# Five features of the last two tiles looked up by one-hot products instead of gathered, and a layer moved behind tile 14

## The reference

```python
e = stack([tbl_f[ids[:, f]] for f in range(26)], axis=1)       # 2048 x 26 x 128
combined = concatenate([dense[:, None, :], e], axis=1)           # 27 vectors a sample
dots = einsum('bfd,bgd->bfg', combined, combined)[:, IU0, IU1]   # its 351 pairs
h = concatenate([dense, dots, dense], axis=1)                    # 607 numbers
h = maximum(h @ W_top1 + b_top1, 0)                              # 512
h = maximum(h @ W_top2 + b_top2, 0)                              # 256
y = h @ W_top3                                                   # 1
```

## Time and profile before

| | us |
|---|---|
| median of 3 runs | 379.87 |
| lowest, highest | 377.62, 384.15 |
| span of the profiled execution, first to last instruction | 496.1 |
| TensorE busy in it | 376.0 |
| VectorE, ScalarE, GpSimd busy in it | 244.4, 195.0, 254.8 |
| mean granted TensorE clock, as a share of full speed | 0.904 |

### The profile page before, as it was taken

The page is one execution under the profiler, slowest core; times in us unless marked ns, Lnnn a source line. Parts: engine busy times, 40 slices in busy tenths (PEclk is TensorE's granted clock), DMA queues, the critical chain, the costliest instruction groups (busy, mean ns, idle before and its releaser), DMA issues.

```text
span 496.1 us, 8109 instructions
## 1 busy us (share of the span) xinstructions
PE 376.0 (76%) x3360; PEld 301.4 (61%) x3360; DVE 244.4 (49%) x174; ACT 195.0 (39%) x261; POOL 254.8 (51%) x266
## 2 busy tenths in 40 slices
PE   1951777858586665978798796969788696879997
PEld 1630656647474554767586666867676455666787
DVE  4740789674919370765725750956566101112133
ACT  3810986414242521525252532434354334344400
POOL 6774540655737363646666554747466564730000
PEclk9985799989989796989998898989899898789899
DMA  8841763259915153456714533536232621123330
GB/s 210 218 134 41 218 187 85 70 156 275 227 29 161 45 155 103 109 150 153 183 46 128 160 87 104 143 93 193 74 89 63 168 73 27 49 63 100 69 71 5
DMA packets 38479, 58.44 MB, mean 118 GB/s; under 512 B 21665, under 2 KB 22561, under 8 KB 38444
## 3 DMA queue, kind: packets, MB, share of 16 engines
q1 hardware_dynamic: 29304, 40.74, 30.3%
q0 software_dynamic: 8192, 16.79, 13.5%
q10 hardware_dynamic: 948, 0.41, 0.4%
HBM read 47.68 MB, written 10.23 MB: 117 GB/s over the span
## 4 chain that ended last, share of the span: by engine, by line
PE 58%; issue 16%; DVE 11%; another core or an unknown queue 8%; SPq 3%; DMA 2%; ACT 2%; DVEq 0%; ACTq 0%
PE look_bank L727 25%; PE short_bank L821 15%; DVE one_hot L1031 8%; PE out_bank L757 6%; PE out_bank L771 4%; PE short_bank L806 4%; PE out_bank L766 3%; SPq L632 2%; DVE all_combined L1044 1%; DVE low_table L1019 1%; DMA spread_ids<-in_ids_by_feature 1%; PE out_bank L783 1%; SPq L621 1%; DMA last_scratch<-all_dots 1%
## 5 line engine op out<-in xcount | busy, mean ns | idle before, releaser
L682 POOL DMA_INDIRECT rows<-in_tbl,all_ids x256 | 253.9, 992 | 191.9 <-PE short_bank L821 81.9
L1031 DVE TENSOR_TENSOR one_hot<-spread_ids,row_bank 128x2048 fp32r<-128x2048 int32 (+3 forms) x80 | 170.7, 2175 | 27.1 <-PE look_bank L727 10.7
L727 PE MATMUL look_bank<-one_hot,high_table 125*128 125x512 f32 x328 | 140.8, 429 | 20.0 <-issue 16.1
L727 PE MATMUL look_bank<-one_hot,low_table 125*128 125x512 f32 x328 | 132.4, 404 | 0.6 <-issue 0.6
L821 PE MATMUL short_bank<-all_combined 128*59 128x54 f32 x2048 | 88.1, 247 | 53.2 <-issue 51.5
L821 PEld LDWEIGHTS short_bank<-all_combined 128*59 128x59 f32 x2048 | 79.7, 162 | 66.7 <-issue 66.5
L1044 DVE COPY all_combined<-short_bank 128x512 f32<-128x512 f32 x32 | 21.8, 691 | 156.2 <-PE short_bank L806 122.3
L727 PEld LDWEIGHTS look_bank<-one_hot,high_table 125*128 125x128 f32 x328 | 64.5, 197 | 40.5 <-issue 23.6
L727 PEld LDWEIGHTS look_bank<-one_hot,low_table 125*128 125x128 f32 x328 | 64.6, 197 | 16.9 <-issue 4.1
L925 ACT COPY all_dots<-short_bank 128x432 f32<-128x432 f32 x64 | 33.1, 518 | 97.1 <-remote 53.7
L878 ACT COPY looked_up<-look_bank 128x512 f32<-128x512 f32 x40 | 23.4, 586 | 120.8 <-remote 45.3
(11 more groups left out here) (42 smaller groups left out, 183.5 us busy)
## 6 DMA issues: line engine op xcount, KB each, us to landing
whole_table<-in_tbl SPq DMA_DIRECT2D x26, 448.0 KB
spread_ids<-in_ids_by_feature SPq DMA_DIRECT2D x40, 256.0 KB
block_scratch<-all_dots SPq DMA_DIRECT2D x24, 208.0 KB
rows<-in_tbl,all_ids POOLq DMA_INDIRECT x256
block_scratch<-all_dots SPq DMA_DIRECT2D x24, 104.0 KB
pairs<-block_scratch SPq DMA_DIRECT2D x72, 29.2 KB
whole_table<-in_tbl SPq DMA_DIRECT2D x26, 52.0 KB
whole_table<-in_tbl SPq DMA_DIRECT2D x2, 560.0 KB
```

What stands on the lines that cost most here:

```text
L682: nc.gpsimd.indirect_dma_start(rows[:, t % ROW_TILES, slot, :], None, tables[SLOT_FEATURES[slot]][:, :], bass.IndirectOffsetOnAxis(ap=all_ ...
L727: last = nc.tensor.matmul(look_bank[s % LOOK_BANKS][:], table_parts[part][TABLE_PLACE[s]][0:ROWS_K, c, :], one_hot[0:ROWS_K, (chunks_befor ...
L1031: last = nc.vector.tensor_tensor(one_hot[:, place:place + n, :], spread_ids[:, s % ID_PLACES:s % ID_PLACES + 1, :].to_broadcast([P, n, COLS]),
```

## The change

Tiles 14 and 15 gather only slots 0 to 10, in groups of 4, 4 and 3. Slots 11 to 15 (five tables of 1250 rows, ten chunks each) become lookups 40 to 44 for these two tiles together, in 256 columns. TensorE does eight of their ten halves behind tile 12 and two behind tile 13. Their tables are loaded, cast and split like the others; ScalarE copies the results into the place of block 2's (`copy_late`) and moves five for tile 14 behind lookup 44, five for tile 15 behind tile 14 (`move_late`), for which the dots of these tiles wait. Of block 2's layers, six steps of layer 1 stay behind tile 12, ten stand behind tile 13, and layer 2 stands behind tile 14, where the last transposes of tile 15 now come before the third layer. The places for ids go from seven to five. The core of the diff:

```diff
-LOOK_FEATURE = [SLOT_FEATURES[GATHERED[m] + LOOK_SLOT[s]] for s, m in enumerate(BLOCK_OF)]
+LATE_LOOKS, LATE_TILES = 5, 2
+ALL_LOOKS = LOOKS + LATE_LOOKS
+LATE_SLOT = GATHERED[LAST] - LATE_LOOKS
+FIRST_LATE = TILES - LATE_TILES
+LATE_COLS = LATE_TILES * P
+LOOK_FEATURE = ([SLOT_FEATURES[GATHERED[m] + LOOK_SLOT[s]] for s, m in enumerate(BLOCK_OF)]
+                + SLOT_FEATURES[LATE_SLOT:GATHERED[LAST]])
...
-ID_PLACES = 7
+ID_PLACES = 5
 LOOK_PLACES = 15
 SPLIT_AHEAD = 2
-AGAIN = [m > 0 and s - FIRST_LOOK[m] < TABLE_PLACES for s, m in enumerate(BLOCK_OF)]
+AGAIN = [m > 0 and s - FIRST_LOOK[m] < TABLE_PLACES for s, m in enumerate(BLOCK_OF)] + [False] * LATE_LOOKS
 TABLE_PLACE = []
-for s, m in enumerate(BLOCK_OF):
-    TABLE_PLACE.append(s if s < TABLE_PLACES else TABLE_PLACE[2 * FIRST_LOOK[m] - 1 - s if AGAIN[s] else s - TABLE_PLACES])
+for s in range(ALL_LOOKS):
+    TABLE_PLACE.append(s if s < TABLE_PLACES else
+                       TABLE_PLACE[2 * FIRST_LOOK[BLOCK_OF[s]] - 1 - s if AGAIN[s] else s - TABLE_PLACES])
 HIGH, LOW = range(2)
-GROUPS = [[4, 4, 4, 4] for _ in range(BLOCKS)]
+GROUPS = [[4, 4, 4, 4]] * FIRST_LATE + [[4, 4, 3]] * LATE_TILES
+assert all(sum(sizes) == (LATE_SLOT if t >= FIRST_LATE else MOST_GATHERED) for t, sizes in enumerate(GROUPS))
...
+LATE_HALVES_AFTER = {LAST * PER_BLOCK: 8, LAST * PER_BLOCK + 1: 2}
+LATE_OUTS_AFTER = [6, 10]
...
-        return [out_steps(LAST - 1)[:12], out_steps(LAST - 1)[12:-1], [],
+        first = 2 * LOOKS + sum(LATE_HALVES_AFTER.get(i, 0) for i in range(t))
+        looks = [step for half in range(first, first + LATE_HALVES_AFTER.get(t, 0)) for step in look_steps(half)]
+        outs, (a, b) = out_steps(LAST - 1)[:-1], LATE_OUTS_AFTER
+        return [merge(looks, outs[:a], 1.0), merge(looks, outs[a:a + b], 0.5), outs[a + b:],
...
-        ahead = ahead[:-1] + out_steps(LAST - 1)[-1:] + out_steps(LAST)[:4] + ahead[-1:]
+        return ahead[:-1] + work_after(t) + ahead[-1:] + out_steps(LAST - 1)[-1:] + out_steps(LAST)[:4]
...
-                sp.dma_start(spread_ids[:, i, :], ids_by_feature[s:s + 1, :].to_broadcast([P, COLS])).then_inc(
+                n = look_cols(s)
+                sp.dma_start(spread_ids[:, i, 0:n], ids_by_feature[s:s + 1, COLS - n:COLS].to_broadcast([P, n])).then_inc(
...
-                if s + TABLE_PLACES < LOOKS and not AGAIN[s + TABLE_PLACES]:
+                if s + TABLE_PLACES < ALL_LOOKS and not AGAIN[s + TABLE_PLACES]:
                     sp.wait_ge(half_done, 2 * (s + 1))
                     load_table(s + TABLE_PLACES)
             def load_ahead(s):
-                if s + ID_PLACES < LOOKS:
+                if s + ID_PLACES < ALL_LOOKS:
...
-                        last = nc.tensor.matmul(look_bank[s % LOOK_BANKS][:], table_parts[part][TABLE_PLACE[s]][0:ROWS_K, c, :],
-                                                one_hot[0:ROWS_K, (chunks_before(s) + c) % HOT_PLACES, :],
+                        last = nc.tensor.matmul(look_bank[s % LOOK_BANKS][:, 0:look_cols(s)], table_parts[part][TABLE_PLACE[s]][0:ROWS_K, c, :],
+                                                one_hot[0:ROWS_K, (chunks_before(s) + c) % HOT_PLACES, 0:look_cols(s)],
...
+                if t >= FIRST_LATE:
+                    pe.wait_ge(late_moved, t - FIRST_LATE + 1)
...
+            def copy_late(s):
+                act.wait_ge(look_moved, moves_by(LAST * PER_BLOCK - 1))
+                act.wait_ge(half_done, 2 * (s + 1))
+                nc.scalar.copy(late_looked_up[:, s - LOOKS, :], look_bank[s % LOOK_BANKS][:, 0:LATE_COLS]).then_inc(look_copied, 1)
+            def move_late(t):
+                u = t - FIRST_LATE
+                act.wait_ge(look_copied, ALL_LOOKS)
+                wait_for_tile(t)
+                nc.scalar.copy(combined[:, :, 1 + LATE_SLOT:1 + LATE_SLOT + LATE_LOOKS],
+                               late_looked_up[:, :, u * P:(u + 1) * P].rearrange("d n p -> d p n")).then_inc(late_moved, 1)
...
+                            if t > FIRST_LATE:
+                                move_late(t)
                         if g % 2 == 1:
                             copy_group(t, g)
                     elif kind == "look":
                         s, = of
+                        if s >= LOOKS:
+                            copy_late(s)
+                            high_part(s + SPLIT_AHEAD)
+                            if s == ALL_LOOKS - 1:
+                                move_late(FIRST_LATE)
+                            continue
...
-                        one_hot[:, place:place + n, :], spread_ids[:, s % ID_PLACES:s % ID_PLACES + 1, :].to_broadcast([P, n, COLS]),
-                        bank_row(CHUNKS[s])[:, c:c + n].unsqueeze(2).to_broadcast([P, n, COLS]), ALU.is_equal)
+                        one_hot[:, place:place + n, 0:cols], spread_ids[:, s % ID_PLACES:s % ID_PLACES + 1, 0:cols].to_broadcast([P, n, cols]),
+                        bank_row(CHUNKS[s])[:, c:c + n].unsqueeze(2).to_broadcast([P, n, cols]), ALU.is_equal)
...
-                for half in range(made, min(made + count, 2 * LOOKS)):
+                for half in range(made, min(made + count, 2 * ALL_LOOKS)):
                     if not by_act(half):
                         make_half(half)
-                return min(made + count, 2 * LOOKS)
+                return min(made + count, 2 * ALL_LOOKS)
...
+                made = make(made, LATE_HALVES_AFTER.get(t, 0))
```

More of the change, by code:

```diff
@@ L127, in group_slots @@
 def group_slots(t, g):
-    sizes = GROUPS[t // PER_BLOCK]
+    sizes = GROUPS[t]
     first = sum(sizes[:g])
@@ L134, in n_groups @@
 def n_groups(t):
-    return len(GROUPS[t // PER_BLOCK])
+    return len(GROUPS[t])
 def groups_by(t):
@@ L181, in loads_by, with look_cols @@
     return sum(TABLE_PLACE[i] == TABLE_PLACE[s] and not AGAIN[i] for i in range(s + 1))
+def look_cols(s):
+    return COLS if s < LOOKS else LATE_COLS
 def look_place(s):
@@ L191, in chunks_before @@
     return sum(CHUNKS[:s])
-HALF_ENDS = [chunks_before(s) + part[-1] + 1 for s in range(LOOKS) for part in halves(s)]
+HALF_ENDS = [chunks_before(s) + part[-1] + 1 for s in range(ALL_LOOKS) for part in halves(s)]
 def runs_of(s, h):
@@ L379, in build @@
         for i in range(TABLE_PLACES):
-            shape = [P, max(CHUNKS[s] for s in range(LOOKS) if TABLE_PLACE[s] == i), D]
+            shape = [P, max(CHUNKS[s] for s in range(ALL_LOOKS) if TABLE_PLACE[s] == i), D]
             with nc.sbuf_tensor(f"whole_table{i}", shape, F32) as whole:
@@ L392, in build @@
         looked_up = sb("looked_up", [P, LOOK_PLACES, COLS])
+        late_places = -(-LATE_LOOKS * LATE_COLS // COLS)
+        assert late_places <= LOOK_PLACES - IN_BLOCK[LAST]
+        late_looked_up = looked_up[:, 0:late_places, :].rearrange("d i p -> d (i p)")[:, 0:LATE_LOOKS * LATE_COLS].rearrange(
+            "d (n p) -> d n p", n=LATE_LOOKS)
         all_combined = sb("all_combined", [P, P * VECTORS + LOADED - SQUARE])
@@ L457, in build @@
         look_moved = sem("look_moved")
+        late_moved = sem("late_moved")
         turned_done = sem("turned_done")
@@ L844, in high_part @@
             def high_part(s):
-                if s >= LOOKS or AGAIN[s]:
+                if s >= ALL_LOOKS or AGAIN[s]:
                     return
@@ L1024, in make_half @@
                 s, h = divmod(half, 2)
+                cols = look_cols(s)
                 if h == 0:
@@ L1149 @@
     a = np.asarray(inputs['ids']).reshape(P, BLOCKS, PER_BLOCK, FEATURES).transpose(1, 3, 2, 0)
-    a = np.ascontiguousarray(a[BLOCK_OF, LOOK_FEATURE].reshape(LOOKS, COLS))
+    a = np.ascontiguousarray(a[BLOCK_OF + [LAST] * LATE_LOOKS, LOOK_FEATURE].reshape(ALL_LOOKS, COLS))
     arrays["in_ids_by_feature"] = a
```

## The result

The changed kernel takes 390.93 us (median of 4 runs, 389.87 to 393.98) against 380.76 for the kernel before beside it: 1.030 times as long, 95% interval 1.023 to 1.037, thus 10 us more. The forecast was 390.4.

What follows compares the result with a forecast made beforehand. The prediction took TensorE alone to carry the end, with the gathers of tiles 14 and 15 hidden. Its terms, -1.3 + 12.2 - 0.5 - 1.5 - 0.8 + 1.1 + 1.0 + 0.3, gave +10.5 us on 379.87: 390.4 us, range 379 to 399.

Steps and rivals of the forecast that it cites:

- (b): TensorE behind tiles 12 and 13: 100 added lookup products at 0.122 us each, +12.2 us (11.5 to 22.9).
- (a): Removed work: ten gathers, 12.9 us of GpSimd, all hidden, worth 0; ten transposes, -1.3 us.
- the gathers' rival: Gathers bind the end without the profiler's gaps; ten fewer save up to 12.9 us, about 369 us; chance 0.10.
- (c): Behind tile 12: lookups fill only 0.5 us of TensorE's wait for low pairs, and the lower clock stays; -0.5 us.
- (g): SP's queue: late tables (12 DMAs), waits ahead of block 2's pair loads and five id places cost 0, each up to +2.
- (d): Moved layer steps add and remove nothing themselves; block 3's wait and clock -1.5, last copy -0.8, layer 2's copy +1.1 us.
- (e): ScalarE before dots 12: table 41's cast now precedes the move of tile 12's last slots, +1.0 us; late moves 0.
- (f): VectorE behind tile 12: ten more one-hots and five splits, 22.6 us; table 43's split late by 0.3 us (0 to 3).
- VectorE and ScalarE bind: Behind tile 12 each lookup waits for one-hot, cast, split and bank: +18, 398 us; chance 0.10 shared with column cost.
- 256 columns cost as 512: Lookup products of 256 columns take as long as 512: +21, 401 us; shares the 0.10 chance with VectorE and ScalarE.
- the lookups land in idle time: Half or more of the 12 us fills TensorE's waits for pairs behind tiles 12 and 14: +2 to +6, 384 us; chance 0.25.

Runs made afterwards that it cites:

- e4: Kernel before, with tiles 14 and 15 gathering only slots 0 to 10 and nothing else changed: 378.50 us, ratio 0.998; its profiled execution took 374.57 us.
- e6: Changed kernel, its five late lookups multiplying only by the high part of their tables (50 of 100 added products left out): 384.33 us, ratio 1.015.
- e1: Kernel before with five places for ids instead of seven, nothing else: 379.61 us, ratio 1.000; its profiled execution took 380.39 us.
- b0: Kernel before, profiled once more without any edit: span 381.0 us, time 382.93 us in one run.
- e3: Changed kernel with the ten gathers put back, into rows that nobody reads: 389.03 us, ratio 1.029.
- e2: Kernel before with layer 2 moved behind tile 14 and tile 15's last transposes ahead of the third layer, all gathers kept: 388.05 us, ratio 1.020.
- e7: Changed kernel with layer 2 back behind tile 13 and the third layer ahead of tile 15's last transposes: 388.93 us, ratio 1.025.
- e5: Changed kernel, SP loading block 2's first pairs and the dense columns before it waits for lookup 37 and loads table 41: 391.58 us, ratio 1.033.
- e13: Kernel before, with the next block's dense columns loaded ahead of the first pairs instead of behind them: 379.74 us, ratio 1.001.
- e8: Changed kernel with lookups 40 and 41 (40 products) ahead of layer 1 behind tile 12: 389.60 us, ratio 1.028.
- e10: Changed kernel with only two late lookups, both ahead of layer 1, layer 2 behind tile 13, pair and dense loads ahead of the late table: 378.39 us, ratio 0.997.
- e12: The two-lookup version with table 41 between stores and pair loads, dense columns first, tile 12's last move ahead of table 41's cast: 378.63 us, ratio 0.997.

## Why the prediction was right, and where its steps were not

The time (390.4 for 390.9) and the sign came out, and so did the main term. That they came out to half a microsecond is luck: errors stood on opposite sides of the sum, some 3 us each against an ordinary execution of the kernel before, some 5 against the fastest of e4.

**Main term (b), right.** The added products stand 0.12 us apart, as taken (0.122). In the changed kernel's timeline of TensorE, the wait for the low pairs, lookups at the lower clock right behind it, and at full clock:

```profile
311.13 0.77 PE L784 MATMUL out_bank<-high_dense,high_w 128*128 128x512 f32 x1 [4.03 <-DVE low_pairs L1128]
...
312.55 0.41 PE L754 MATMUL look_bank<-one_hot,high_table 125*128 125x256 f32 x1
312.76 0.41 PE L754 MATMUL look_bank<-one_hot,low_table 125*128 125x256 f32 x1
...
324.42 0.29 PE L754 MATMUL look_bank<-one_hot,high_table 125*128 125x256 f32 x1
324.54 0.28 PE L754 MATMUL look_bank<-one_hot,low_table 125*128 125x256 f32 x1
```

At the lower clock they are 0.21 us apart (312.55 to 312.76), at the higher 0.12. The e6 run removed half of the products and 5.8 us. The Trainium skill ("TensorE: Matmul & The Clock Gate", Back-to-back issue gap) has 262 cycles for an isolated product of 256 columns, by estimate 0.109 us; here, with a weight load for each product, it is 0.120, and the measurement decides.

**The bound, and term (a), wrong.** "The gathers of tiles 14 and 15 are thus hidden by some 15 us" fails. I took the gaps in the dots as a cost of that execution and subtracted them for TensorE, but left GpSimd's slack as it stood, though the gathers wait for the dots and had only idled because the dots were late. 78 us of gaps taken from one engine's time take slack from all that waits for it. Nor was the "against" of the gathers' rival sound: I priced 256 gathers at 0.99 + 0.3 us; without the gaps they have a mean of 1.036, 342 us with what lies between them; the last one starts at 345, and from its end to the end of the span it is 35 us, where I had put 31. The rival said that it decides 15 us from what was shown; that is about where the kernel before stands. Its condition was true, and its price of up to 12.9 us was not, because something else is late within microseconds: fewer gathers alone gave 1.2 us at the medians (ratio 0.998, interval 0.994 to 1.001) and 5 us in the one execution that was profiled (dots 12 to dots 15 in 44.5 us instead of the 49.5 of e1). I had taken 0.

**Terms (c) and (g), mis-sized.** Take e4's execution first, since nothing waits for gathers in it. Against its 44.5 us the changed kernel needs 59.2. The ten transposes that e4 keeps add 1.3 to that difference: 16.0 us for what the prediction put at 12.2 - 0.5 - 1.5 - 0.8 + 1.1 + 0.3 = 10.8. The wait for the low pairs wasn't filled by 0.5 us but stands at 4.03, against 2.97 in e4 and 2.46 in b0: its end is 8.3 us behind dots 12 instead of 6.8 (e4), since the pair loads end later (304.97 in the changed kernel, 302.23 in the e1 profile). That is +1.5 for (g), for which I took 0, up to +2. And behind the wait TensorE runs at the lower clock, the next 16 lookup products and six products of layer 1 with it, where e4's 36 products took 8.46 us, at full clock: another 2.7 us by the spacing (16 x 0.09 + 6 x 0.2). The 1.3 us of clock at block 3's first products that (d) gave back is no gain against e4, which had no slow stretch there (6 products in 1.56 us, where the earlier trace rows has 2.83). It isn't to be had where the clock is up anyway. The three make 5.5 us for the 5.2 that are missing.

But e4's is the fastest of ten executions. Against e1's the same stretch is 59.2 for 49.5, 9.7 us longer, where the prediction had 9.5. There the low pairs are wanted 6.6 us behind dots 12 (+1.7 for (g)), the 36 products take 10.0 us, 1.6 of it from the lower clock, as in the earlier trace rows (+1.1, not 2.7), and block 3's first six products take 2.5 us, so (d)'s gain was real. These 2.8 us are balanced by what the gathers cost in that execution, of which a wait of 1.0 us for rows in tile 14's transposes is one part. How large (g) and (c) are varies by the execution, too. In e3, whose TensorE does what the changed kernel's does, the wait for the low pairs is 2.5 us and ends 7.0 behind dots 12, and the stretch takes 56.4 us. So the direction of the errors stands on single executions, and their size is open by some 3 us. A slip that costs nothing here: the late tables and their ids are 15 DMAs, not the 12 of term (g).

**Term (d), half right.** The order of events is as told. Layer 2 at its new place, its copy, and what follows, in the chain of the changed kernel:

```profile
346.42 6.88 PE out_bank L798 x16
353.33 1.18 ACT hidden L981
354.64 1.92 PE out_bank L810 x16
...
358.39 3.61 PE short_bank L850 x128
```

The 16 instructions of layer 2 take 6.88 us; ScalarE's copy of 1.18 us stands ahead of the third layer, as the +1.1 said; block 3's first eight instructions take 1.84 at full clock; and dots 15 follow with no wait. But "adds and removes nothing by itself" holds only with fewer gathers: e2 shows 8 us for the move alone, e7 some 2 us at the medians for it beside the lookups. I hadn't asked what layer 2 covered where it stood.

**Term (e), right (0.8 for 1.0).** Between the copy of look 39 and the move of tile 12's last slots now stands the cast of table 41 (the answer to the earlier trace rows), and before that a wait of 10 us for the dense columns:

```profile
290.70 0.43 ACT L950 COPY all_combined<-dense_cols 128x128 f32<-128x128 f32 x1 [10.05 <-DMA dense_cols<-in_r_dense_features]
...
296.73 0.59 ACT L907 COPY looked_up<-look_bank 128x512 f32<-128x512 f32 x1
297.21 1.26 ACT L881 CAST high_table<-whole_table 125x1280 fp32r<-125x1280 f32 x1
298.37 0.50 ACT L940 COPY all_combined<-looked_up 128x256 f32<-128x256 f32 x1
```

The move ends at 298.87 and dots 12 start at 299.13, 0.77 us later than TensorE was ready. The wait of 10 us cost nothing that a run shows: e5 shortened it by 3 us for no gain, and e13 removed the 6 us of it that the kernel before has, for 0.

**Term (f), right in size** (0.3 us taken, and behind the low pairs no wait for VectorE in the changed kernel), but e6 and e8 show that it has no reserve: with fewer products, or with the first wait filled, VectorE's split comes to the front.

**Rivals.** "VectorE and ScalarE bind" and "256 columns cost as 512" are out by the rows above, and e6 agrees; "the lookups land in idle time" is out for five of them, and true for two (e10). Of the stretches that the prediction named as its test, dots 12 to dots 13 grew by 6.8 us against b0 where it had 4 to 6, and dots 14 to dots 15 by 3.3 where it had 4 to 5. What stays open: e4's one profiled execution is faster than its median by 4 us, and the runs don't tell which wait comes and goes between its executions.

## What to carry to other kernels

When a profiled execution is far longer than the runs, its gaps can't be subtracted from one engine alone: whatever waits for that engine has slack in the profile that the runs don't have, so look for an undisturbed profile, or take the same microseconds from every slack before calling work hidden. Before a piece of work is moved, ask what it covered where it stood, for DMAs as well as engines. And a trade of one engine's work for another's near balance is worth only the difference to the next late thing: here some 1 to 5 us of gathers against 12 us of products.

## What the runs showed of the hardware that was not expected

The disturbed execution had a span of 496.1 us, and the later profile of the same kernel 381.0: the 128 small products of a tile took up to 14.5 us in it while gathers ran, and 3.7 to 5.2 in the other.

TensorE's lower level came in behind the wait of 4.0 us in the changed kernel (lookups 0.21 us apart) and the one of 2.46 us in b0 (granted clock 0.81 in that stretch), while in e4, behind 2.97 us, the 36 products took 8.46 us, all at the higher one. The length of the wait alone doesn't tell these apart.

The two DMAs of a table (the larger of 560 KB), issued right ahead of eight stores, moved their landing from 2.9 to 5.4 us behind the last issue (e5; 4.9 in e10), and issued behind them left it at 2.9 (e12). I take the start of the pair loads, which wait for the stores, for the landing.

Without the gaps the mean gather takes 1.036 us where the undelayed one takes 0.94: some 24 us of GpSimd over the 256. In b0's trace 33 gathers take over 1.0 us. Of these, 32 start while VectorE runs an operation with two inputs in SBUF, nearly all of them splits, and end 0.81 to 0.83 us behind it, as in the earlier trace rows; they hold 23.5 of the 24 us. Of the gathers that overlap such an operation but start first (or in its last 0.02 us), all 25 take 0.94 or 0.95 us. The Trainium skill ("SBUF — State Buffer", Who interferes with whom) says that such a two-input operation keeps GpSimd's reads out, and the rows agree. No run took the splits away.
